# Causal masks of the relative stage moved from TensorE to VectorE and GpSimd, and the pieces between stages spread wider in the radial and rotary intervals

## The reference

```python
x = x + _L0_attn_a_ref(_layernorm(x), ...)   # masked: softmax over keys i[None, :] >= i[:, None]
x = x + _L0_ffn_ref(_layernorm(x), ...)
x = x + _L0_attn_b_ref(_layernorm(x), ...)   # radial: exp(-sigma * |q - k|^2), no softmax
x = x + _L0_ffn_ref(_layernorm(x), ...)
x = x + _L1_attn_a_ref(_layernorm(x), ...)   # relative: scores = q.k + u.k + _rel_shift((q + v).r)
x = x + _L1_ffn_ref(_layernorm(x), ...)
x = x + _L1_attn_b_ref(_layernorm(x), ...)   # rotary: q and k rotated by position, softmax
x = x + _L1_ffn_ref(_layernorm(x), ...)
```

## Time and profile before

| | |
|---|---|
| median of 3 runs | 2918.95 us (2916.05 to 2922.97) |
| the profiled execution | 2915.31 us, its span 2913.2 us |
| granted TensorE clock | 0.99 of full speed over the span |
| busy over the span | PE 2717.3 us (93%), VectorE (DVE) 2061.4 us (71%), ScalarE (ACT) 2132.1 us (73%), GpSimd (POOL) 752.8 us (26%) |
| chain that ended last | PE 67%, VectorE 22%, issue 5%, ScalarE 3% |
| where the stages lie | copies of radial heads (L1212) 586.8 to 1099.7 us, upper-form products of the relative stage (L799) 1103.8 to 2125.8 us, the masked stage before and the rotary one behind |

### The profile page before, as it was taken

One profiled execution on the slowest core, in us unless ns is written; L12 is line 12 of the kernel. 1 busy time (PEld: TensorE's weight loads), 2 busy tenths in 40 slices (PEclk: granted clock), 3 DMA queues, 4 the chain that ended last, 5 costly groups with the idle time before them and its releaser, 6 DMA issues.

```text
span 2913.2 us, 106272 instructions
## 1 busy us (share of the span) xinstructions
PE 2717.3 (93%) x43868; PEld 1622.8 (56%) x44000; DVE 2061.4 (71%) x4743; ACT 2132.1 (73%) x3765; POOL 752.8 (26%) x1365
## 2 busy tenths in 40 slices
PE   4999999999999999999999999999999999999895
PEld 2666665655555556666666666566644444444443
DVE  3888888631221237777777877778779989899893
ACT  1777776789999986666666666566668878788784
POOL 3312223240312423401610340140023141141101
PEclk9999999999999999999999999999999999999997
DMA  6323233343323432311321331222123222232211
GB/s 174 104 81 113 83 115 89 109 134 94 116 79 120 128 112 86 103 48 47 120 61 48 95 103 46 72 86 60 40 64 96 60 87 72 72 101 59 80 53 32
DMA packets 197914, 250.79 MB, mean 86 GB/s; under 512 B 48228, under 2 KB 113892, under 8 KB 197432
## 3 DMA queue, kind: packets, MB, share of 16 engines
q1 hardware_dynamic: 197432, 244.00, 28.1%
HBM read 133.51 MB, written 100.14 MB: 80 GB/s over the span
## 4 chain that ended last, share of the span: by engine, by line
PE 67%; DVE 22%; issue 5%; ACT 3%; SPq 1%; DMA 1%; POOL 1%; ACTq 0%; DVEq 0%; POOLq 0%
PE ppv L949 27%; DVE mx L1203 16%; PE ring L809 6%; PE ring L858 5%; PE ring L793 5%; PE ring L820 3%; PE ring L891 3%; PE pm L980 2%; DVE seen L1198 2%; PE ring L849 2%; ACT probs L1084 1%; PE ring L907 1%; PE pm L1024 1%; PE pm L1033 1%; ACT xn L1092 1%
## 5 line engine op out<-in xcount | busy, mean ns | idle before, releaser
L1084 ACT ACTIVATE probs<-ring 128x512 f32<-128x512 f32 (+1 forms) x3280 | 1998.8, 697 | 711.6 <-PE ring L809 210.0
L1203 DVE TENSOR_REDUCE mx<-ring 128x1 f32<-128x512 f32 (+2 forms) x2112 | 1287.5, 650 | 234.8 <-PE ring L858 77.5
L949 PE MATMUL ppv<-probs,values 128*32 128x128 f32 x30208 | 1154.8, 278 | 5.4 <-DVE osb L1212 2.5
L949 PEld LDWEIGHTS ppv<-probs,values 128*32 128x32 f32 x30208 | 789.6, 109 | 333.2 <-issue 179.3
L1198 DVE CUSTOM_DVE_ANT_0 seen<-ring,low_seen 128x512 f32<-128x512 f32 x576 | 393.5, 683 | 125.4 <-PE ring L858 124.8
L865 PE MATMUL ring<-kst,qst 48*128 48x512 bf16 (+1 forms) x1060 | 365.2, 391 | 41.4 <-DVE mx L1203 20.9
L1427 POOL CAST mparts<-mall 128x8 bf16<-128x8 f32 x192 | 37.0, 193 | 1254.0 <-DVE mall L1221 959.9
L820 PE MATMUL ring<-qst,kst 51*128 51x512 bf16 (+2 forms) x1092 | 344.8, 385 | 3.3 <-ACT probs L1084 2.7
L858 PE MATMUL ring<-kst,qst 112*128 112x512 bf16 (+3 forms) x768 | 251.0, 327 | 0.9 <-DVE mx L1203 0.9
L809 PE MATMUL ring<-qst,kst 115*128 115x512 bf16 (+3 forms) x768 | 250.7, 326 | 0.1
L901 PE MATMUL ring<-kst,qst 48*128 48x512 bf16 x732 | 209.4, 328 | 16.3 <-DVE mx L1203 16.2
(11 more groups left out here) (141 smaller groups left out, 2903.7 us busy)
## 6 DMA issues: line engine op xcount, KB each, us to landing
qst<-records_q SPq DMA_DIRECT2D x448, 96.0 KB
heads_out<-osb SPq DMA_DIRECT2D x256, 128.0 KB, 2.1
kst<-records_k SPq DMA_DIRECT2D x320, 96.0 KB
records_k<-parts SPq DMA_DIRECT2D x96, 256.0 KB, 3.2
records_q<-parts SPq DMA_DIRECT2D x96, 256.0 KB, 3.3
kst<-records_k SPq DMA_DIRECT2D x128, 102.0 KB
oT<-heads_out SPq DMA_DIRECT2D x64, 128.0 KB, 2.6
den<-inverses SPq DMA_DIRECT2D x48, 128.0 KB, 2.6
```

What stands on the lines that cost most here:

```text
L949: mm = pe.matmul(ppv[32 * g:32 * g + 32, c:c + P], values[:, (n // H) % 2, v:v + 32], src[:, at * P:(at + 1) * P], start=u == 0 and qt < 4 ...
L1084: nc.scalar.activation(probs_of(rd.n, u), src, ACT.Exp, scale=1.0 if rd.s == RBF else SCALE).then_inc(s_exp, 1)
L1203: ins = dve.tensor_reduce(mx[:, slot, to:to + 1], bank[:, at * P:(at + nt) * P], AX.X, ALU.max)
```

## The change

Six edits.

- In the relative stage the two masks of the upper form leave TensorE. In the direction of the maxima VectorE applies it: four `tensor_tensor_reduce` of 128 columns with `up_seen` (one 128x128 table) instead of one reduction of 512. In the other direction the scores go unmasked through the exponential, and GpSimd then sets the hidden part of the probabilities to zero (`hide_upper`, an `affine_select` in place on a tile of 128x512), for unit 8 in slot 9 and for unit 17 in slot 0 of the next round. `take_values` waits for it at units 8 and 17.
- `lag` of the relative stage: the bursts are now units 0 to 4 after slot 6, 5 to 7 after 10, 8 to 12 after 14, 13 to 17 after 20.
- `take_out` after a relative head comes in slot 3.
- `bank` frees `pm` after `APART` ticks: 3 as before in masked and relative intervals and in the last radial one, 6 in the other three radial intervals, 9 in the rotary ones.
- `norm` gives a tile of `xn` every second tick in rotary intervals.
- The tables `up_qk` and `up_kq` are replaced by `up_seen`.

```diff
@@ -150,7 +150,7 @@
     if rd.wide:
         return {u + 3: [u, u + 1] for u in range(0, n, 2)}
     if rd.s == REL:
-        return {6: [0, 1, 2, 3, 4], 10: [5, 6, 7, 8], 14: [9, 10, 11, 12], 19: [13, 14, 15, 16, 17]}
+        return {6: [0, 1, 2, 3, 4], 10: [5, 6, 7], 14: [8, 9, 10, 11, 12], 20: [13, 14, 15, 16, 17]}
     if n == 9:
         return {5: [0, 1, 2], 8: [3, 4, 5], 11: [6, 7, 8]}
     return {5: [0, 1], 6: [2, 3], **{u + 4: [u, u + 1] for u in range(4, n, 2)}}
@@ -179,6 +179,11 @@
 OP_US = {MASKED: SPLIT_US * 2, RBF: (1.3,) + SPLIT_US * 2 + (0.7, 1.2, 0.7, 1.2), REL: SPLIT_US * 2 + (2.4,) + ((2.5,) * 3 + SPLIT_US) * 2,
          ROPE: (2.5,) * 6 + SPLIT_US * 2}
 GROUPS = {MASKED: (3, 7), RBF: (4, 8, 12), REL: (3, 7, 15, 22), ROPE: (9, 13)}
+
+
+
+APART = {MASKED: 3, RBF: 6, REL: 3, ROPE: 9}
+TILES_APART = {MASKED: 1, RBF: 1, REL: 1, ROPE: 2}
 
 
 def interval_of(f):
@@ -226,7 +231,7 @@
         tick = max(tick, self.free)
         self.at[("fill", *name)] = tick
         self.at[("take", *name)] = tick + 1
-        self.free = tick + 3
+        self.free = tick + self.apart
         return tick + 1
 
     def norm(self, j, i, w, tick, steps):
@@ -235,12 +240,14 @@
             self.at["stat" + w, j, i, t] = tick + t
         tick = self.pool(("pool", j, "dev" + w, i), self.later(tick + NT, 1.0), 3.0)
         for t in range(NT):
-            self.at["xn" + w, j, i, t] = tick + t
-        return [tick + 3 + 2, tick + 7 + 2]
+            self.at["xn" + w, j, i, t] = tick + t * self.tiles
+        return [tick + t * self.tiles + 2 for t in (3, 7)]
 
     def lay(self, j):
         at, i = self.at, j + 1
         self.j, self.us, self.taken = j, US[j // B], set()
+        self.apart = 3 if j == REL * B - 1 else APART[j // B]
+        self.tiles = TILES_APART[j // B]
         base = ROUNDS[H * j].tick
         self.free = base
         late = [f for f in range(INTERVALS) if interval_of(f) == j]
@@ -305,7 +312,7 @@
 
         i, at = j + 1, self.at
         s = min(i, INTERVALS - 1) // B
-        self.free = tick
+        self.free, self.apart = tick, 0
         names = [(j, i, "ta", 0), (j, i, "ta", 1)] + [(j, i, "pr", n) for n in range(2 * PROJ[s])] + \
             [(j, i, "va", 0), (j, i, "va", 1)]
         w = "a"
@@ -447,8 +454,7 @@
         low_seen = sb("low_seen", [P, 8 * P], BF16)
         seen = sb("seen", [P, 3, HALF])
         low_kq = sb("low_kq", [P, P + 1], BF16)
-        up_qk = sb("up_qk", [P, HALF], BF16)
-        up_kq = sb("up_kq", [P, HALF], BF16)
+        up_seen = sb("up_seen", [P, P], BF16)
 
         ring = ps("ring", [P, 6, HALF])
         ppv = ps("ppv", [P, HALF])
@@ -472,6 +478,7 @@
         s_sm = sem("s_sm")
         s_mf = sem("s_mf")
         s_mp = sem("s_mp")
+        s_up = sem("s_up")
         s_zc = sem("s_zc")
         s_zd = sem("s_zd")
         s_ze = sem("s_ze")
@@ -728,7 +735,7 @@
             const1(neghalf[:, :], k["neghalf"])
             const1(zmask[:, :], k["zmask"])
             const1(heads_of[:, :], k["heads_of"])
-            for dst, n in ((low_seen, "low_seen"), (low_kq, "low_kq"), (up_qk, "up_qk"), (up_kq, "up_kq")):
+            for dst, n in ((low_seen, "low_seen"), (low_kq, "low_kq"), (up_seen, "up_seen")):
                 const1(dst[:, :], k[n].bitcast(BF16))
             for n in range(4):
                 const1(tables[:, n], k["tables"][n])
@@ -796,9 +803,8 @@
                     rows = slice(0, ROW + BASE + 3)
                     if upper(unit):
                         for i, (kt, qt, _, at) in enumerate(unit):
-                            pe.matmul(bank[:, at * P:(at + 1) * P], keys[rows, slot, kt * P:(kt + 1) * P],
-                                      qst_up[rows, slot, qt * P:(qt + 1) * P], start=i == 0, stop=False)
-                        mm = pe.matmul(bank[:, :], identb[:, :], up_kq[:, :], start=False, stop=True)
+                            mm = pe.matmul(bank[:, at * P:(at + 1) * P], keys[rows, slot, kt * P:(kt + 1) * P],
+                                           qst_up[rows, slot, qt * P:(qt + 1) * P], start=i == 0, stop=i == len(unit) - 1)
                     else:
                         (kt, q0, nt, _), = unit
                         lo, hi = q0 * P, (q0 + nt) * P
@@ -846,9 +852,8 @@
                     rows = slice(0, ROW + BASE)
                     if upper(unit):
                         for i, (qt, kt, _, at) in enumerate(unit):
-                            pe.matmul(bank[:, at * P:(at + 1) * P], qst_up[rows, slot, qt * P:(qt + 1) * P],
-                                      keys[rows, slot, kt * P:(kt + 1) * P], start=i == 0, stop=False)
-                        mm = pe.matmul(bank[:, :], identb[:, :], up_qk[:, :], start=False, stop=True)
+                            mm = pe.matmul(bank[:, at * P:(at + 1) * P], qst_up[rows, slot, qt * P:(qt + 1) * P],
+                                           keys[rows, slot, kt * P:(kt + 1) * P], start=i == 0, stop=i == len(unit) - 1)
                     else:
                         (qt, k0, nt, _), = unit
                         lo, hi = k0 * P, (k0 + nt) * P
@@ -933,6 +938,8 @@
                         j = n // H
                         pe.wait_ge(s_pc, FILL["fill", j - 1, j, "va", 1] + 1)
                 src, final = probs_of(n, u), u == len(rd.kq) - 1
+                if rd.s == REL and upper(rd.kq[u]):
+                    pe.wait_ge(s_up, 2 * (n - REL * HEADS) + (2 if final else 1))
                 if final and rd.s == REL:
                     pe.wait_ge(s_zv, n - REL * HEADS + 1)
                     for t in range(NT):
@@ -1161,7 +1168,7 @@
                 for u in range(rd.slots):
                     if u < len(rd.kq):
                         exponential(rd, u)
-                    if u == 2 and rd.n > 0 and stage(rd.n - 1) != RBF:
+                    if u == (3 if stage(rd.n - 1) == REL else 2) and rd.n > 0 and stage(rd.n - 1) != RBF:
                         take_out(rd.n - 1)
                     if u == rd.slots // 2 and soft(rd.n + 1) and stage(rd.n + 1) == REL:
                         m = rd.n + 1 - REL * HEADS
@@ -1184,9 +1191,12 @@
                 bank = ring[:, item % 3]
                 dve.wait_ge(s_s, item + 1)
                 if stage(n) == REL and upper(unit):
-                    to = 2 * NT + unit[0][0]
-                    dve.tensor_reduce(mx[:, slot, to:to + 4], bank[:, :].rearrange("p (t q) -> p t q", t=4), AX.X, ALU.max)\
-                        .then_inc(s_sm, 1)
+                    dve.wait_ge(s_sm, item - 2)
+                    for qt, _, _, at in unit:
+                        to = 2 * NT + qt
+                        ins = dve.tensor_tensor_reduce(seen[:, item % 3, at * P:(at + 1) * P], bank[:, at * P:(at + 1) * P], up_seen[:, :],
+                                                       1.0, 3.0 * BIG, ALU.add, ALU.max, mx[:, slot, to:to + 1])
+                    ins.then_inc(s_sm, 1)
                 elif len(unit) == 2 and unit[0][2] == unit[1][2]:
                     to, end = unit[0][0], NT + unit[1][0]
                     dve.tensor_reduce(mx[:, slot, to:end + 1:end - to], bank[:, :].rearrange("p (t q) -> p t q", t=2), AX.X, ALU.max)\
@@ -1449,6 +1459,12 @@
                 pool.tensor_tensor(zvals[:, i % 2, 0:HCOLS].rearrange("p (t e) -> p t e", t=NT),
                                    after[:, slot].rearrange("p (t e) -> p t e", t=NT),
                                    zexp[:, i % 2].unsqueeze(2).to_broadcast([P, NT, VCOLS]), ALU.mult).then_inc(s_zv, 1)
+
+            def hide_upper(n, u):
+
+                pool.wait_ge(s_exp, ROUNDS[n].exps + u + 1)
+                tile = probs_of(n, u).rearrange("p (t q) -> p t q", t=4)
+                pool.affine_select(tile, tile, [[0, 4], [-1, P]], ALU.is_ge, 0.0, base=-2, channel_multiplier=1).then_inc(s_up, 1)
 
             def next_scores(n):
@@ -1590,6 +1606,10 @@
             for rd in ROUNDS.values():
                 m = rd.n + 1
                 for u in range(rd.slots):
+                    if u == 0 and rd.n > 0 and stage(rd.n - 1) == REL:
+                        hide_upper(rd.n - 1, 17)
+                    if u == 9 and rd.n >= 0 and rd.s == REL:
+                        hide_upper(rd.n, 8)
                     if u == 1:
                         if rd.turn >= 0:
                             split_max(m)
@@ -1655,8 +1675,7 @@
         "hide_kq": np.concatenate([hide(i[:, None] % ROW + ROW * n < i[None, :]) for n in range(2)], 1),
         "low_seen": hide((band[None, :] > i[:, None]) & ((band[None, :] < P) | (band[None, :] == P) & (i[:, None] == P - 1))),
         "low_kq": hide((wide[None, :] - 1 < i[:, None]) & ((wide[None, :] > 0) | (i[:, None] == 0))),
-        "up_qk": np.tile(hide(i[None, :] < i[:, None] + 2), (1, 4)),
-        "up_kq": np.tile(hide(i[:, None] < i[None, :] + 2), (1, 4)),
+        "up_seen": hide(i[None, :] < i[:, None] + 2),
         "zmask": np.where((i[:, None] == P - 1) & (np.arange(NT)[None, :] == NT - 1), f(BIG), f(0)).astype(f),
```

## The result

| | before | after |
|---|---|---|
| median, measured in turns | 2918.39 us (4 runs) | 2881.85 us (4 runs, 2876.30 to 2889.84) |
| ratio | | 0.9875, 95% interval 0.9844 to 0.9906 |
| the profiled execution | 2915.3 us | 2876.3 us |

The account below looks back on a forecast made before the run. The prediction took TensorE to bound relative heads, ScalarE and TensorE radial ones, VectorE rotary ones. Terms of -52, -4 and -18 us gave -74 us, hence 2845 us against the 2918.95 us median; range 2820 to 2880 us.

Parts of the forecast that it names:

- Term 1: Relative stage: masks leave TensorE, 256 x 0.22 = 56 us saved, 4 us lost once in head 178; -52 us.
- the stall in head 178: Relative stage: the mask of unit 8 queues behind a GpSimd operation waiting for swapped projections; +4 us, once.
- rivals A and B: Relative stage. A: nothing overlaps on VectorE, 2884 us, chance 0.08. B: GpSimd's mask is late, 2889 us, 0.06; slower, 0.04.
- I set the two equal: Relative heads: TensorE's new 0.2 us wait at slot 2 taken as equal to the vanished 0.19 us before the transposed maximum.
- TensorE is the bound: Relative stage: TensorE busy 88.4 of 90.2 us in plain heads, so all 256 masks of 0.22 us count, 56 us.
- Term 2: Three radial intervals with pieces six slots apart: odd pieces become even, -1.2 us an interval, -4 us; ends 0 and -12.
- the distance itself buys little: Radial intervals: the slot's parity, not the spacing, prices a piece; the lone even piece still costs 0.31 us.
- The low end of -12: Radial term's far end: half of all piece cost saved, -12 us over three intervals.
- Term 3: Rotary intervals: spread tiles and pieces save 4.5 us in each of three intervals and 4.5 in the last; -18 us.
- cost nothing: Radial and rotary stages: GpSimd's operations and stores move some 30 slots later with the pieces, at no cost.
- Rival C: Radial and rotary stages: the spread does nothing, pieces cost what they did; -52 alone, 2867 us, chance 0.12.

Follow-up runs that it names:

- e1: The kernel before with only the masks moved to VectorE and GpSimd, other parts of the change undone; 2881.95 us, ratio 0.9871 to the kernel before.
- e11: The changed kernel with VectorE's masked units replaced by the former single unmasked reduction of 512 columns, so that mask is missing; 2857.84 us, ratio 0.9810.
- e13: The changed kernel with both GpSimd masks of the relative stage and the waits for them left out; 2876.53 us, ratio 0.9853.
- e14: The changed kernel with GpSimd's scaling of the turned output moved to slot 28 in relative intervals; 2870.39 us, ratio 0.9855.
- e4: The changed kernel with second statistics 11 slots and ff pieces 6 slots later in three rotary intervals, behind the turns; 2867.28 us, ratio 0.9833.
- e5: The changed kernel with the relative stage's normalised tiles two slots apart instead of one; 2881.10 us, ratio 0.9884.
- e7: The changed kernel with the pieces of three radial intervals four slots apart instead of six; 2884.95 us, ratio 0.9896.
- e10: The changed kernel with the pieces of three relative intervals six slots apart instead of three; 2872.15 us, ratio 0.9846.
- e3: The changed kernel with rotary normalised tiles one a slot again, pieces still nine slots apart; 2903.21 us, ratio 0.9951.
- e15: The change with old burst and take-out, e4 and e6 edits, scaling at slot 28, first rotary statistics five slots later; 2877.11 us, ratio 0.9852.
- e9: The changed kernel with GpSimd's scaling of the turned output moved to slot 24 in relative intervals; 2877.75 us, ratio 0.9864.
- e6: The changed kernel with GpSimd's operations on the swapped projections at slot 58 instead of 44 in the last relative interval; 2869.35 us, ratio 0.9831.
- e2: The changed kernel with the rotary part taken back: pieces every third slot, tiles every slot; 2877.55 us, ratio 0.9868.

## Why the prediction was wrong

**Term 1, -52 forecast, -29.4 measured.** Right were the 0.22 us of a mask, the 0.21 us of a short reduction and 0.88 us for a plain head (0.87 in e1), the stall in head 178 (3.0 us, 4 forecast) and rivals A and B as unlikely. Failed is the step "I set the two equal": the new wait at slot 2 costs 0.07 us a head more than the old one at the turn (e1), 3 us in 38 plain heads. The step that failed by far is the one that priced piece-laden heads like plain ones. Head 1 was expected at -0.88 us and came at +1.05, +1.03, +2.47 and +2.14, together 10.2 us from the forecast. In that head VectorE is the bound up to the turn: what leaves TensorE is worth nothing there, and the masked unit that falls in it is paid in full (e1, e11). The earlier trace rows are of plain heads only, and "TensorE is the bound" was carried from them to all. Of the 1.03 us by which head 1 of the second interval grew, GpSimd's mask is 0.34 (e13), VectorE's masked units are 0.24 (e11) and the shift is 0.23 (e1); the other 0.22 was not taken apart. In two of the four heads GpSimd's scaling beside the tiles came on top, 3.3 and 3.0 us (e14), of which the kernel before had 1.8 and 1.9 (its heads 1 took 20.53 and 20.62 us there, 18.69 elsewhere). Heads 0, 3, 7 and 8 gave 8.5 us less than 0.88 each; which engine holds each of them was not tried.

**Term 2, -4 forecast, -10.5 measured in three intervals.** The step "the distance itself buys little" failed. It rested on one lone piece at 777.46, whose 0.31 us of wait I took for the whole price. The run of intervals from three to seven slots shows 1.4, 1.3, 1.0 and 0.7 us for each slot. The low end of -12 was the nearer one.

**Term 3, -18 forecast, +1.2 measured.** The spread does shorten an interval where the turns are kept clear, by less than was forecast: -2.8 us in e4, -4.5 forecast. What failed is "cost nothing" for what moves with the pieces. I followed GpSimd's operations and the stores, but not the second statistics and the addition to x, both on VectorE, which the planner places behind the last piece. They landed ahead of the turns at 117 and 197, and ahead of them they cost 4.9 us an interval in the changed kernel's profile (e4), with 10.2 us of half clock; in the executions that had only 3.4 us of it (e5, e7, e10) the interval was 184.5, and they cost 1.5. The stores did not cost here, but e3 and e15 show that this was the luck of their place: where the swaps of the projections come a few slots earlier or later in the same queue, TensorE waits 5.3 and 4.4 us. Rival C (2867 us) had this term at nothing, as it came, but for the wrong reason: its pieces cost what they did, and here a gain and a new cost cancel.

## What to carry to other kernels

A price read in plain rounds holds only there: before multiplying by the number of rounds, look in each kind of round which engine has no wait. When a table moves some work, list all that is placed relative to it, on every engine and in the DMA queue, and see which of it lands just ahead of a point where engines meet, or ahead of a load that one of them waits for; in these runs such a wait was often paid twice, since TensorE's clock was at half after it. GpSimd work is free only beside VectorE instructions that it does not hold up.

## What the runs showed of the hardware

A two-input GpSimd operation on 128x1024 holds a VectorE `tensor_scalar` of 128x128 that starts during it until it ends: 2.23 us instead of 0.34 (changed kernel, e9), and a mask of 0.635 us holds it for 0.68. VectorE's reductions from the banks of `ring` that start during the same operations kept their time, 0.29 us for a masked one of 128 columns and 0.68 us for 512. The Trainium skill, "SBUF — State Buffer", section "Who interferes with whom", says that copies and `tensor_scalar` in a two-port mode and GpSimd fully block each other, the one that starts first having its way, and that reductions never contend. The traces agree, with 2.23 and 0.68 us; the mode itself shows in none of them. Applied to the order of time it gives head 1 its 0.34 us.

In head 7 of the changed kernel TensorE had waited 0.42 and 0.46 us, was busy 0.78 of the 1.7 us from 2364.0 on, and had just begun its wait of 0.56 us when the granted clock went to 0.50, for 6.8 us. In e6 three waits of the same lengths were followed by 3.4 us at half, from 1.2 us behind the last of them. In other runs of the same code it stayed at half for 3.4 or 10.2 us (e7, e5), or did not fall (head 12: 12.28 us with a fall, 10.90 without). On the way from the radial to the relative stage head 14 takes 15.9 us in most executions, but 25.8 in the profiled ones of e2, e13 and e15, with the clock at half for 24 to 34 us: 10 to 14 us of difference between executions, as wide as the spread of most kernels here, and not explained.
